# Keys of a Perceiver block in matmuls of 512 columns: context in chunks of 512 tokens, with a new order of the head

## What is computed

```python
k = heads(key, Wk, bk, Sk)                                    # 12544 x 512 times 512 x 512
v = heads(value, Wv, bv, Sk)                                  # 12544 x 512 times 512 x 512
k_prime = jax.nn.relu(jnp.einsum('bhnd,fd->bhnf', k, Wkf))    # 32 -> 64 features per head
k_prime = k_prime * attention_mask[:, None, :, None]
kv = jnp.einsum('bhnf,bhne->bhfe', k_prime, v)                # summed over all tokens
k_sum = jnp.sum(k_prime, axis=2)
out = qkv / (qk_sum + 1e-08)
```

## Time and profile before

| | us |
|---|---|
| median of 3 runs (922.66 to 926.15) | 925.56 |
| the profiled execution | 923.34 |
| its span, first to last instruction | 921.3 |
| PE busy | 903.2 (98%) |
| DVE busy | 646.8 (70%) |
| ACT busy | 558.5 (61%) |
| POOL busy | 357.4 (39%) |

### The profile page before, as it was taken

The page is one execution under the profiler, slowest core; times in us unless marked ns, Lnnn a source line. Parts: engine busy times, 40 slices in busy tenths (PEclk is TensorE's granted clock), DMA queues, the critical chain, the costliest instruction groups (busy, mean ns, idle before and its releaser), DMA issues.

```text
span 921.3 us, 16856 instructions
## 1 busy us (share of the span) xinstructions
PE 903.2 (98%) x5590; PEld 761.2 (83%) x5590; DVE 646.8 (70%) x1183; ACT 558.5 (61%) x1061; POOL 357.4 (39%) x164
## 2 busy tenths in 40 slices
PE   6999999999999999999999999999999998999998
PEld 4899999999999999999999999999999997444443
DVE  3777777777777777777777777777777776532422
ACT  3577777777676777777777777776767664111000
POOL 1345454545454545454545454545444442000000
PEclk8999999999999999999999999999999999999999
DMA  6121211212121211010101010101010101803900
GB/s 207 68 72 63 73 64 73 71 66 75 62 82 54 86 51 68 23 46 23 46 23 46 23 46 23 46 23 46 23 46 23 46 1 65 373 0 141 406 1 11
DMA packets 14316, 63.99 MB, mean 69 GB/s; under 512 B 2016, under 2 KB 3808, under 8 KB 13280
## 3 DMA queue, kind: packets, MB, share of 16 engines
q1 hardware_dynamic: 13296, 61.48, 18.1%
q10 hardware_dynamic: 1008, 2.35, 0.7%
HBM read 63.56 MB, written 0.26 MB: 69 GB/s over the span
## 4 chain that ended last, share of the span: by engine, by line
PE 90%; issue 6%; DVE 2%; DMA 1%; ACT 1%; POOL 0%; SPq 0%; POOLq 0%; DVEq 0%; ACTq 0%
PE k_bank L517 11%; PE k_bank L518 10%; PE k_bank L519 10%; PE kv_ps L570 10%; PE f_ps L560 10%; PE v_bank L517 10%; PE v_bank L518 10%; PE v_bank L519 9%; PE kv_ps L730 3%; PE v_bank L627 2%; PE k_bank L627 2%; DMA ctx_raw<-in_ctx 1%; PE k_bank L613 1%; DVE kf L836 0%; PE f_ps L618 0%
## 5 line engine op out<-in xcount | busy, mean ns | idle before, releaser
L319 POOL TENSOR_TENSOR ksum_acc<-ksum_acc,kf 128x1024 f32<-128x1024 f32 x97 | 233.5, 2407 | 289.0 <-DVE kf L831 285.1
L806 DVE SCALAR_TENSOR_TENSOR keys<-k_bank,bias_cols,keys 64x256 fp32r<-64x256 f32 x392 | 189.6, 484 | 91.1 <-ACT keys L388 86.9
L517 PE MATMUL k_bank<-ctx_hi,wk_lo 128*128 128x256 f32 x784 | 231.8, 296 | 5.8 <-POOL ctx_lo L335 4.9
L407 ACT ACTIVATE fb<-f_ps 128x256 f32<-128x256 f32 x392 | 150.1, 383 | 142.7 <-PE f_ps L560 132.4
L518 PE MATMUL k_bank<-ctx_lo,wk_hi 128*128 128x256 f32 x784 | 222.5, 284 | 0.0
L519 PE MATMUL k_bank<-ctx_hi,wk_hi 128*128 128x256 f32 x784 | 222.2, 283 | 0.0
L388 ACT ACTIVATE keys<-k_bank,bias_cols 64x256 fp32r<-64x256 f32 x392 | 184.0, 469 | 41.3 <-PE k_bank L519 37.6
L824 DVE TENSOR_TENSOR kf<-f_ps,fb 128x256 f32<-128x256 f32 x392 | 164.2, 419 | 58.6 <-ACT fb L407 55.4
L517 PEld LDWEIGHTS k_bank<-ctx_hi,wk_lo 128*128 128x128 f32 x784 | 150.4, 192 | 32.0 <-DVE keys L806 24.3
L312 POOL TENSOR_TENSOR ctx_lo<-ctx_raw,ctx_hi 128x1024 fp32r<-128x1024 f32 x48 | 115.6, 2409 | 119.0 <-ACT ctx_hi L380 119.0
L560 PE MATMUL f_ps<-bd,keys 128*128 128x256 f32 x784 | 157.1, 282 | 2.5 <-DVE kf L824 2.5
(11 more groups left out here) (150 smaller groups left out, 727.7 us busy)
## 6 DMA issues: line engine op xcount, KB each, us to landing
ctx_raw<-in_ctx SPq DMA_DIRECT2D x49, 512.0 KB, 3.3
early<-in_early SPq DMA_DIRECT2D x22, 512.0 KB, 4.3
w_out<-in_wout SPq DMA_DIRECT2D x1, 4096.0 KB, 14.2
fc<-in_fc SPq DMA_DIRECT2D x1, 4096.0 KB, 24.9
early<-in_proj SPq DMA_DIRECT2D x1, 4096.0 KB, 13.5
early<-in_fc SPq DMA_DIRECT2D x1, 4096.0 KB, 22.8
w_out<-in_proj SPq DMA_DIRECT2D x1, 4096.0 KB, 21.8
early<-in_wk SPq DMA_DIRECT2D x2, 512.0 KB, 8.8
```

Of the source, the lines that this page charges most:

```text
L319: pool.tensor_tensor(ksum_acc[:, :].rearrange("p (j f) -> p j f", f=P), ksum_acc[:, :].rearrange("p (j f) -> p j f", f=P), kf[:, t, :, :], ...
L407: act.activation(fb[:, i % 2, :, :], f_ps[i % 2][:, :].rearrange("p (j x f) -> p j x f", j=2, x=2) [:, :, 1, :], ACT.Copy).then_inc(fb_rea ...
L517: pe.matmul(out_ps, st_lo, mv_hi, start=start, stop=False, **kw)
L806: last = dve.scalar_tensor_tensor(out=keys_2[other, s, 2 * g + h, :], in0=k_bank[rows, (g % 2) * CHUNK:(g % 2 + 1) * CHUNK], scalar=bias_c ...
```

## The change

A chunk now has 512 tokens. It is loaded in two halves of 256 tokens (`HALF`), each into the one `ctx_raw`, and split in quarters of one tile (128 tokens) by ACT and by POOL, one per tile. A tile makes one key block m of the next chunk (12 matmuls of 512 columns) in place of two blocks of 256 columns; four tiles make the four blocks. `keys_high` and `keys_low` become two instructions each of 64 partitions by 512, and DVE's first waits only for ACT's first. There are 24 chunks of 512 and a last one of 256, whose keys are made in matmuls of 256 columns (`n_keys`). In the last two tiles the first one's values go to `k_bank`.

The head has another order: weights `wk` and two halves of context are loaded first, then `wv`, `x`, `ident` and `wq`, nearly all by SP. All four key blocks of chunk 0 are made before the queries, into four different banks (`k_first`), as 96 matmuls of 256 columns; the query features (8 matmuls) stand inside the values of tile 0. The splitting of `wv` is shared by DVE and POOL. `wk` lies block by block in memory.

The second half of `w_swiglu` (4 MB, `swi_b`) is no longer loaded in the loop but in the tail, between `w_o` and `w_out`; 14 pieces are left in the loop. `proj0` is asked for after the second `u` product, not the fourth. The steady loop has two chunks of four tiles per pass, so half as many passes and twice the code.

```diff
-CHUNK = 256
+HALF = 256
+CHUNK = 2 * HALF
...
-EARLY = SWI_AT + KC * 2 * DFF
+EARLY = SWI_AT + SWI_HALF
...
             for b in range(2):
-
-                sp.dma_start(wk_raw[:, :, b * CHUNK:(b + 1) * CHUNK], wk_in[:, :, b * CHUNK:(b + 1) * CHUNK])\
-                  .then_inc(wk_loaded[b], 16)
+                ms = slice(2 * b, 2 * b + 2)
+                sp.dma_start(wk_raw[:, ms, :, :], wk_in[:, ms, :, :]).then_inc(wk_loaded[b], 16)
                 if b == 0:
                     sp.dma_start(ctx_raw[:, :, :], ctx_in[0, :, :, :]).then_inc(ctx_loaded, 16)
+                    sp.dma_start(ctx_raw_b, ctx_in[1, :, :, :]).then_inc(ctxb_loaded, 16)
+            sp.dma_start(wv_raw, wv_in).then_inc(wv_loaded, 16)
+            sp.dma_start(x_sb[:, :], x_in).then_inc(x_loaded, 16)
             sp.dma_start(ident[:, :], ident_in).then_inc(ident_loaded, 16)
+            sp.dma_start(wq, wq_in).then_inc(wq_loaded, 16)
...
+            def load_half(h):
+
+                sp.wait_ge(ctx_lo_ready, 2 * h - 2)
+                sp.dma_start(ctx_raw[:, :, :], ctx_in[h, :, :, :]).then_inc(ctx_loaded, 16)
...
-            def split_ctx_low(c, s):
-
-                pool.wait_ge(ctx_hi_ready, c + 1)
-                pool.tensor_tensor(ctx_lo[:, s, :, :], ctx_raw[:, :, :], ctx_hi[:, s, :, :].bitcast(f32),
-                                   ALU.subtract).then_inc(ctx_lo_ready, 1)
+            def split_ctx_low(g, s, t):
+
+                pool.wait_ge(ctx_hi_ready, g - 1)
+                cols = slice(t * P, (t + 1) * P)
+                pool.tensor_tensor(ctx_lo[:, s, :, cols], ctx_raw[:, :, t % 2 * P:(t % 2 + 1) * P],
+                                   ctx_hi[:, s, :, cols].bitcast(f32), ALU.subtract).then_inc(ctx_lo_ready, 1)
...
+            def keys_high(c, s, m, src, n):
+
+                act.wait_ge(k_done, KC * c + m + 1)
+                for h in range(2):
+                    rows = slice(PAIR * h, PAIR * (h + 1))
+                    act.activation(keys_2[rows, s, 2 * m + h, 0:n], src[rows, 0:n], ACT.Identity,
+                                   bias=bias_cols[rows, KC + m:KC + m + 1]).then_inc(k_hi_ready, 1)
...
+            def keys(c, s, m, jobs, n=CHUNK):
+
+                pe.wait_ge(ctx_lo_ready, TILES * c + n // P - 2)
+
+                pe.wait_ge(k_lo_ready, 2 * (KC * c + m))
+                for k in range(KC):
+                    last = three(k_bank[:, 0:n], wk_hi[:, m, k, :], wk_lo[:, m, k, :],
+                                 ctx_hi[:, s, k, 0:n], ctx_lo[:, s, k, 0:n], k == 0, k == KC - 1)
                     if k == KC - 1:
-                        last.then_inc(v_done, 1)
-                    if all_jobs or k % 2 == 0:
-                        feature_job(*beside, k if all_jobs else k // 2)
+                        last.then_inc(k_done, 1)
+                    if k % 2 == 0:
+                        feature_job(*jobs[k // 2])
...
+            def period(c, s, n_keys=CHUNK):
                 n = TILES * c
                 for t in range(TILES):
+                    jobs = [(c, s, n + t, t, i) for i in range(JOBS)]
+                    values(n + t, s, t, jobs[0:2])
+                    keys(c + 1, 1 - s, t, jobs[2:4], n_keys)
+                    key_values(n + t - 1, t + 1)
...
+            def values_last(n, s, t, jobs):
+
+                if t == 0:
+                    pe.wait_ge(k_lo_ready, 2 * KC * (LAST + 1))
+                else:
+                    pe.wait_ge(v_lo_ready, n - 1)
+                for k in range(KC):
+                    value_step(n, s, t, k, k_bank if t == 0 else v_bank)
+                    feature_job(*jobs[k])
...
+            def keys_low(c, s, m, src, n):
+
+                for h in range(2):
+                    dve.wait_ge(k_hi_ready, 2 * (KC * c + m) + h + 1)
+                    rows, other = slice(PAIR * h, PAIR * (h + 1)), slice(PAIR * (1 - h), PAIR * (2 - h))
+                    dve.scalar_tensor_tensor(
+                        out=keys_2[other, s, 2 * m + h, 0:n], in0=src[rows, 0:n],
+                        scalar=bias_cols[rows, KC + m:KC + m + 1],
+                        in1=keys_2[rows, s, 2 * m + h, 0:n].bitcast(f32), op0=ALU.add, op1=ALU.subtract)\
+                       .then_inc(k_lo_ready, 1)
```

More of the change, by code:

```diff
@@ L347, in _ @@
             pool.wait_ge(rms_eps_set, 1)
[L348 removed]
+            period(LAST, 0, last=True, splits=0)
             pool.wait_ge(tail_small_loaded, 16 * 4)
@@ new lines, in features_high, with tile @@
+                act.activation(kf_2[:, t % 2, :, 0, :], kf[:, t % 2, :, :], ACT.Copy).then_inc(kf_hi_ready, 1)
+            def tile(n, t, first=False, last=False, last_tile=False, keys=(), splits=()):
+                features_share(n, 0, first and t == 0)
+                if not (first and t == 0):
+                    features_high(n - 1, t - 1)
+                features_share(n, 1, first and t == 0)
+                if last:
+                    features_share(n, 2, False)
+                    features_share(n, 3, False)
+                if last_tile:
+                    features_high(n, t)
+                values_high(n, t, first, k_bank if last and t == 0 else v_bank)
+                for x in splits:
+                    split_ctx_high(*x)
+                if not last:
+                    features_share(n, 2, False)
+                    features_share(n, 3, False)
+                for k in keys:
+                    keys_high(*k)
@@ L443, in split_wk_high, with period @@
+            def period(c, s, last=False, splits=TILES, keys=CHUNK):
+                n = TILES * c
+                for t in range(LAST_TILES if last else TILES):
+                    tile(n + t, t, last=last, last_tile=last and t == LAST_TILES - 1,
+                         keys=() if last else ((c + 1, 1 - s, t, k_bank, keys),),
+                         splits=((2 * c + 4 + t // 2, s, t),) if t < splits else ())
             def split_wk_high(b):
-                cols = slice(b * CHUNK, (b + 1) * CHUNK)
+                ms = slice(2 * b, 2 * b + 2)
@@ L859, in _, with tile @@
-            dve.wait_ge(x_loaded, 16)
-            layer_norm(1, z0, x_sb[:, :], z0_ready)
-            for b in range(2):
-                if b == 1:
-                    dve.wait_ge(ctx_hi_ready, 1)
-                    dve.tensor_tensor(ctx_lo[:, 0, 0:KC // 2, :], ctx_raw[:, 0:KC // 2, :],
-                                      ctx_hi[:, 0, 0:KC // 2, :].bitcast(f32), ALU.subtract)\
-                       .then_inc(ctx0_lo_ready, 1)
-                cols = slice(b * CHUNK, (b + 1) * CHUNK)
+            def tile(n, t, first=False, last=False, last_tile=False, keys=()):
+                features_sum(n, t, 0, first)
+                if not (first and t == 0):
+                    features_low(n - 1, t - 1)
+                features_sum(n, t, 1, False)
+                if first and t == 0:
+                    queries_out()
+                if not last:
+                    values_low(n, t)
+                for i in range(2, JOBS):
+                    features_sum(n, t, i, False)
+                masked_features(n, t)
+                if last_tile:
+                    features_low(n, t)
+                if last:
+                    values_low(n, t, k_bank if t == 0 else v_bank)
+                for k in keys:
+                    keys_low(*k)
@@ new lines, in period, with queries_out @@
+            def period(c, s, last=False, keys=CHUNK):
+                n = TILES * c
+                for t in range(LAST_TILES if last else TILES):
+                    tile(n + t, t, last=last, last_tile=last and t == LAST_TILES - 1,
+                         keys=() if last else ((c + 1, 1 - s, t, k_bank, keys),))
+            def queries_out():
+                for b in range(2):
+                    dve.wait_ge(qf_done, b + 1)
+                    dve.tensor_scalar(qf_T[:, 4 * b:4 * b + 4, :], kv_bank[b].rearrange("p (k t) -> p k t", k=4),
+                                      0.0, None, ALU.max).then_inc(qf_ready, 1)
```

419 lines of the change are left out of this document (209 added, 210 removed).

## The result

The changed kernel takes 898.6 us (median of 4 runs, 897.81 to 899.67), the kernel before 924.48 (median of 4, 922.66 to 926.15): the ratio is 0.9719, with a 95% interval of 0.9704 to 0.9735, so 2.8% faster. Forecast were 895.0 (894 to 897 for a median), with 889 to 908 as the range. The profiled execution took 898.03 us with a span of 896.2, against 923.34 and 921.3 before: 25.1 us of span to be explained, where the sum had 28.4. Two of the eleven runs of the kernel before that stood beside the first experiments (1109.23 and 1795.65 us) were in a slow state and are in no ratio.

A forecast was written before the change was run, and what follows sets the result against it. PE bounds the kernel at 7.634 us per tile, with a stall of some 0.1 us from k_bank's handover. Gains of 19.3 (loop), 6.1 (last chunk's keys) and 3.0 (head) make 28.4 from 923.34: 895 us, range 889 to 908.

The forecast's parts named there:

- The steady loop: 92 tiles with keys of 512 columns: beat 7.42 us for 7.634, 0.21 less per tile, 19.3 us gained.
- the forecast's two prices: Per tile: k_bank's handover stall, some 0.1 us, and the width, 0.229 per 512-column matmul against 0.240 for two of 256.
- The rule on the gap between matmuls: Gap of N/2.4 + 2.5 ns: about 3 us saved over 1104 wide key matmuls, where the trace's prices give 12.
- The last chunk's keys: Four tiles of chunk 23 make 12 key matmuls of 256 columns instead of 24: 6.1 us gained.
- The head: Start to the end of tile 1: keys follow the warm-up at 8.7 at full clock; 3.0 us gained, bounds -2 to 7.
- values of tile 0 start at 24.5: Head: after keys from 8.7 (11.5 us), transposes (0.5) and queries (3.84), values start at 24.5 instead of 28.57.
- 0.6 of waits: Head, to tile 1's end: waits behind context halves 2, 3 and 4, 0.6 us within the forecast end of 40.8.
- The last two tiles: Values in k_bank must wait for the last read-out, 1.5 us of stall; counted as nothing, range -1 to +1.5.
- The tail: Same work as before; swi_b there by 795, wanted at 825.4; no gain or loss.
- Wide keys did cost less: Rival: a 512-column context matmul costs as much as two, or the handover stall stays; 907 us, chance 0.08.
- The quarters did not come late: Rival: context loads turn round in more than 7.42 us and ACT waits; 12 us lost, 907, chance 0.08.
- Instructions were not fetched again: Rival: the longer loop refetches instructions at each back edge, ten passes of 3.3 us, 33 us, 928; chance 0.09.

The follow-up runs named there:

- the two experiments on it: Kernel before with ACT reading k_bank by partition half, signalling each: 914.55 us; changed kernel with each 512-column key matmul made as two of 256: 909.03 us.
- With both removed: Changed kernel with POOL's half of the wv splitting held until z0 is written, and context halves 4 and 5 asked for before SP's qf_done wait: 895.56 us.
- with the wait added: Changed kernel with POOL's half of the wv splitting held until DVE has written z0: 896.01 us, ratio 0.97 to the kernel before.

## Why the prediction was right, and where its sizes were off

**The steady loop** (forecast 92 x 0.21 = 19.3) was right in mechanism and size. The beat is 7.42 to the last digit, and the two experiments on it split the gain into 0.094 for the handover and 0.12 for the width, where the forecast's two prices had 0.08 to 0.1 and 0.13. The read-out was estimated at 0.69 for ACT's and 0.75 for DVE's instruction; they took 0.685 and 0.749. The spare time in `k_bank`'s handover was put at 1.3 us and is 1.4.

**The rule on the gap between matmuls**, from the Trainium skill, page "TensorE: Matmul & The Clock Gate", section "Back-to-back issue gap", would have given 3 us for the width. The experiment with narrow keys measured 10.8 us of loop (and 10.4 in the medians) with nothing but the width changed. The span says 12.3 (908.5 against 896.2), but 1.7 of that is its slower tail. The prediction's own price, 0.240 against 0.229, gave 12 and was a little high: the beats say 0.010 per matmul. The rule fell short because it was asked for something it isn't said to cover. The section gives the formula for a matmul by itself and adds that in a stream of matmuls with a weight load each, as here, it doesn't hold; its own figure for such a stream, about 131 ns at 512 columns, isn't what these rows show either (229).

**The last chunk's keys** (forecast 6.1): the tiles with 256 columns take 6.09 to 6.13 for 7.634, as worked out. Both terms together gave 25.4 where 25.0 had been worked out.

**The head** (forecast 3.0, bounds -2 to 7) was mis-sized: 0.55 measured in the cut that the forecast put at 3.4. Its first half was right, PE's keys at 8.81 for 8.7 and at full clock (that the two agree to 0.1 is luck: in the other profiles with this head the first key stands between 8.4 and 9.6). The window from 9 to 12 us has PE busy without a break at 1.00 (engines' busy us in order, then PEclk, DMA share and GB/s):

```profile
9.00:12.00 3.00, 3.00 (x25) 2.79 (x24) 1.70 (x2) 1.81 (x3) 1.51 (x1) 1.00 1.03 404
```

The step that failed is "values of tile 0 start at 24.5". It added up PE's own work (keys, transposes, queries) and took everything that feeds the queries as done by then. On the chip `x` landed at 13.6, since it now stood in the queue behind the key weights, two halves of context and `wv`. `z0` then lost 2.1 us beside POOL's instruction, DVE's key read-outs and the copy of `z0_T` stood behind it, and PE stood idle for 0.42 us ahead of the transposes and for 1.39 us ahead of the queries, waiting for that copy. With `z0` at 0.73 the queries end at 24.8, 0.3 from the forecast, with `x` still landing at 13.4. Whether `x` at the front of the queue would do the same was not tried. The second part, "0.6 of waits", was nearly right: from the values' start at 27.14 to the end of tile 1 at 43.65 are 16.5 us for the 15.7 that the forecast's sum has without waits, so 0.8, nearly all of it behind half 4. With both removed, tile 1 ends at 41.1 (40.13 + 0.95), against the 40.8 forecast, so this cut gains 3.1 us of the 3.4 in the form that the forecast described.

**The last two tiles** (forecast nothing, -1 to +1.5) cost 0.9 us. The prediction had named the stall of 1.5 and let it be offset by waits of the kernel before. The stall was 1.44, the offset only 0.5. The trace of before shows that offset: in the first of its two tiles PE waited 1.28 us for DVE's feature sums, where the changed kernel, already held at the tile's start, waited only 0.70 (at 741.81):

```profile
765.49 0.47 PE L560 MATMUL f_ps<-bd,keys 128*128 128x256 f32 x2 [0.38 <-DVE kf L824]
766.86 0.50 PE L560 MATMUL f_ps<-bd,keys 128*128 128x256 f32 x2 [0.90 <-DVE kf L824]
```

The second tile's wait, 1.26 us, is the same in both.

**The tail** moved by 0.1 us. `swi_b` was loaded in 14.1 us and nothing waited for it or for the loads behind it.

**The rivals.** Wide keys did cost less and the handover kept no stall. The quarters did not come late: POOL's took 1.31 us, near the lower end of the 1.2 to 2.4 allowed for, and ACT's quarters waited for `ctx_raw` three times, all in the head, and not once in the loop. The waits of ACT for it after, us in all, times and the longest:

```profile
ACT ctx_hi L405 <- DMA ctx_raw<-in_ctx: 7.1, 3, 3.5
```

Instructions were not fetched again. In 300 to 640 us, more than five passes of the longer loop, the only queue with packets was that of the data:

```profile
q1 hardware_dynamic: 3312, 12.06, 10.8%
```

Single pieces of instructions came between 20 and 120 us, up to the end of the loop's first pass; then there were none until 660, behind the loop's end. No tile was longer for it. So a two-page window, outside of which a taken branch stalls (the Trainium skill, page "Runtime: NRT & Kernel Launch", section "Instruction fetch mechanics"), isn't borne out by this loop, which has 320 matmuls and 320 weight loads on PE in a pass; the room for 2048 instructions on PE that the same section names would be in keeping with it.

Left open: the head's terms other than `z0` and half 4 were not taken apart further, and so what the later place of `x` in the queue costs by itself.

## What to carry to other kernels

When a beat of equal length runs through most of the span, price its parts by distances between starts of neighbours in one period, at each width that the period holds; two such prices and one stall forecast what 700 us of this kernel gained within 0.5 us. A head or an end is not priced that way: there every engine's queue has to be walked through, with each instruction that stands ahead of the one that feeds the bound, since a 2.4 us instruction given to an idle engine cost another engine 2.1 us, on an operand whose load had been moved back until it had no slack left. And gains of single edits in a head add up only if each removes a delay that the other leaves standing.

## What the runs showed of the hardware

DVE and POOL held each other up where both worked from SBUF to SBUF, and the one that started second lost about what the first had still to run. DVE's `z0` started at 15.46, when POOL's `wv_lo` had 2.34 us left (15.39 to 17.80), and took 2.81 us for 0.73, so it lost 2.08. The other way round, with the wait added, POOL's `wv_lo` started at 16.01 beside a subtraction of DVE that ended at 17.07, 1.06 later, and took 3.32 instead of 2.41: 0.91 lost. In the changed kernel's tile 1 DVE's `kf` starts with 0.54 left of POOL's sum and takes 1.62 (1.21 in the kernel before at 39.87): 0.41 lost.

```profile
37.60 2.40 POOL L335 TENSOR_TENSOR ksum_acc<-ksum_acc,kf 128x1024 f32<-128x1024 f32 x1 [0.63 <-DVE kf L906]
39.46 1.62 DVE L912 TENSOR_TENSOR kf<-kf 128x1024 fp32r<-128x1024 f32 x1
40.43 1.80 POOL L328 TENSOR_TENSOR ctx_lo<-ctx_raw,ctx_hi 128x512 fp32r<-128x512 f32 x1 [0.43 <-ACT ctx_hi L405]
```

DVE's reading of `k_bank` in PSUM was not stretched: 1.53 us for two from 303.49 on, with POOL's sum running from 303.54 to 305.95 in that tile, and that one took its usual 2.41. The Trainium skill, page "Advanced Engine Details and Errata", section "Mode Summary", says that "The second Vector SBUF port is shared with GPSIMD, so GPSIMD instructions and 2p Vector instructions will interfere/block eachother". The rows agree that the two block each other; which of DVE's instructions are of that 2p kind they don't show. How much is lost, the rest of the first one's time, is what they add.

A weight load held for a bank costs PE about 0.1 us: the first key matmul stood 0.22 from its neighbour instead of 0.12, and removing the hold alone brought the beat from 7.634 to 7.54.
